# Two narrow attentions of a four-layer block: one opening stage instead of two, rows restacked through memory, dummy matmuls at the head

## The chip, the cores and the metric

The kernel runs on one core of a Trainium2 chip. Its time is the device time of one execution in microseconds (us); lower is better. Five engines work side by side: TensorE (PE, matmuls into PSUM), VectorE (DVE), ScalarE (ACT), GpSimd (POOL) and SyncE (SP), which here issues nearly all the transfers. They wait for one another on semaphores; transfers (DMAs) run on the core's 16 DMA engines.

## The reference, cut to what matters

Four layers follow one another on x (8 batches, 256 rows, 128 columns); each is an attention over a context of 64 rows and then a feed-forward part with experts. The change touches the attentions of layers 0 and 2 alone, which have 16 heads of depth 8:

```python
z = layernorm(x)                       # 2048 rows of 128
q = z @ wq + bq                        # 8 x 256 x 128
k, v = ctx @ wk + bk, ctx @ wv + bv    # 8 x 64 x 128
p = softmax(q_h @ k_h.T / sqrt(8) + mask)   # for each of 16 heads; only layer 0 has a mask
x = x + concat_h(p @ v_h) @ wo + bo
```

## The kernel before

The program is a row of blocks. All engines meet at the end of a block; a block ends when each engine has issued its last instruction, and for SP that is the issue of its last DMA, not its landing.

**Normalisation** (`normalise`): DVE takes the statistics of 16 tiles of 128 rows (L134 to L145), ACT the roots, DVE writes normalised tiles in four groups of four (L167), TensorE transposes them (L228), and ACT copies them into `zT` (L202). Layer 0 has then a small block for the context, the mask and converted constants (L2704 to L2745).

**Projection and restacking** (`project_small`): TensorE makes k for all batches and q in four groups of 512 columns (L327, L330), then v (L333). A value is carried as a high part in a rounded format and a low part, the rest: ACT writes the high part (L341, L344), DVE the low part (L350, L355). So that one matmul adds three products, high and low parts must lie one above the other on 96 partitions, for each subset of four heads. SP restacks them with DMAs from on-chip memory to on-chip memory of 32 rows by 512 columns (64 KB) each, line L308: four subsets by three parts make 12 for k and 12 for each group of q, 60 in all. They go out one by one on SP's queue.

**Attention** (`attend_small`): a new block. DVE first clears and fills constant parts (`zeroed`, L561 to L573), and TensorE and ACT wait for it. POOL spreads k of a batch over a block pattern `kbd` (L407) and adds the output bias to x (L413). Then, for batch b, TensorE runs a schedule written out by hand: scores (L423 with the mask of layer 0, L427), from which DVE takes row maxima (L580); the maxima are turned (L437) and written by ACT into rows 96 to 127 of q (L517); the turned scores (L449, L453) come out less their maxima, and ACT exponentiates them (L526); values (L466) of batch b-2 run beside that; DVE divides (L596, L598), TensorE turns and projects (L474, L478), DVE adds to x (L606). Batch b waits for the restacked q of its group (`q_there`), and for its `kbd`.

Of the kernel before, what the change touches and what calls it, by code (L numbers as in the profile page):

```python
# [21 lines left out]
P = 128  # L22
# [251 lines left out]

class Stacked:
# [7 lines left out]
    def __init__(self, m):  # L283
# [4 lines left out]
        self.k_there = m.sem("k_there")  # L288
        self.q_there = [m.sem(f"q_there{g}") for g in range(GROUPS)]


def project_small(nc, tag, w, zT, ctx2T, st, v2_all):

    with ExitStack() as stack:
        m = Memory(nc, stack, tag)
        pq = [m.ps(f"pq{i}") for i in range(GROUPS)]
        pk = m.ps("pk")
        pv = m.ps("pv", 1024)
        q_done, k_done, v_done, k_high_ready, k_low_ready, q_high_ready, q_low_ready = (
            m.sem(n) for n in ("q_done", "k_done", "v_done", "k_high_ready", "k_low_ready", "q_high_ready",  # L300
                               "q_low_ready"))
        block = stack.enter_context(nc.Block())

        @block.sync
        def _(sp):
            def restack(out, src, cols, row, there):
# [4 lines left out]
            every = slice(0, B * KEYS)  # L311
            sp.wait_ge(k_high_ready, 1)
            restack(st.k, st.k_high, every, 0, st.k_there)
            restack(st.k, st.k_high, every, 64, st.k_there)
            sp.wait_ge(k_low_ready, 1)
            restack(st.k, st.k_low, every, 32, st.k_there)
            for g in range(GROUPS):
                cols = slice(g * 512, (g + 1) * 512)
                sp.wait_ge(q_high_ready, g + 1)
                restack(st.q, st.q_high, cols, 0, st.q_there[g])  # L320
                restack(st.q, st.q_high, cols, 32, st.q_there[g])
                sp.wait_ge(q_low_ready, g + 1)
                restack(st.q, st.q_low, cols, 64, st.q_there[g])

        @block.tensor
        def _(pe):
            nc.tensor.matmul(pk[:, :].rearrange("p (b k) -> p b k", k=KEYS), w["wk"][:, :], ctx2T[:, :, 0, :],  # L327
                             start=True, stop=True).then_inc(k_done, 1)
            for g in range(GROUPS):
                nc.tensor.matmul(pq[g][:, :], w["wq"][:, :], zT[:, g * 512:(g + 1) * 512],  # L330
                                 start=True, stop=True).then_inc(q_done, 1)
# [2561 lines left out]
```

## Time and profile before

| | us |
|---|---|
| median of 3 runs | 1666.53 |
| lowest and highest run | 1655.84, 1669.77 |
| profiled execution, its own time | 1663.92 |
| its span, first to last instruction | 1662.1 |

TensorE is busy for 77% of the span, DVE for 60%, ACT for 43%, POOL for 37%; the mean granted TensorE clock is 0.84 of full speed. Two stretches are of interest: from 0 to 152 us the opening and the attention of layer 0, and from 907 to 1062 us the same of layer 2. In a row of the timeline the first number is the start in us from the span's start, the second how long the group lasted; xN counts instructions; the bracket tells how long the engine was idle before, and what released it. One matmul on plain f32 operands is recorded as two.

### The profile page before, as it was taken

To read this page: it belongs to the slowest core of one execution; us is meant where nothing else is said; L and a number is where in the kernel's file an instruction comes from. 1 tells how busy PE (TensorE), PEld (TensorE's weight loads), DVE (VectorE), ACT (ScalarE), POOL (GpSimd) and SP (SyncE) were. 2 spreads that over 40 slices of the span, in tenths; PEclk is the share of its full clock that TensorE was granted. 3 is DMA by queue.
4 is the path that set the end of the run, shared out by engine and by line. 5 is a ranking of instruction groups with operands and counts; after the bars stand their busy time and mean duration, and the time that the engine had idled before them with its cause. 6 is when DMAs were issued, how large, how long until landed. Compare 5 with 4: busy or idle time off the path is not lost. (4 is left out here: it accounts for less than half of the span.)

```text
span 1662.1 us, 24143 instructions
## 1 busy us (share of the span) xinstructions
PE 1282.1 (77%) x7118; PEld 1055.1 (63%) x7118; DVE 995.0 (60%) x2089; ACT 722.9 (43%) x1277; POOL 614.7 (37%) x566
## 2 busy tenths in 40 slices
PE   3297569998897899704994269699966549999997
PEld 2296348987654599703883159578854437787876
DVE  4255668887425377552665143568767776677775
ACT  2043446666332555322562123355542225555554
POOL 0231454432000133164331031149945306666765
PEclk9598869999798899856997555789985659999998
DMA  4530011110000000231112300022212106444433
GB/s 96 170 54 1 1 34 38 38 38 5 1 1 0 20 1 0 76 102 44 47 47 56 79 16 1 20 78 83 82 58 79 40 4 141 116 125 117 127 117 103
DMA packets 75841, 93.63 MB, mean 56 GB/s; under 512 B 16346, under 2 KB 42333, under 8 KB 75754
## 3 DMA queue, kind: packets, MB, share of 16 engines
q1 hardware_dynamic: 73154, 87.85, 18.9%
q0 software_dynamic: 2272, 4.24, 0.8%
q8 instruction: 38, 0.62, 0.2%
q10 hardware_dynamic: 336, 0.59, 0.1%
q14 instruction: 41, 0.34, 0.1%
HBM read 70.01 MB, written 8.92 MB: 47 GB/s over the span
## 5 line engine op out<-in xcount | busy, mean ns | idle before, releaser
L2485 POOL TENSOR_TENSOR e_h<-e_h,e_gate 128x512 f32<-128x512 f32 x128 | 188.1, 1487 | 144.6 <-DVE e_h L2537 87.3
L2542 DVE TENSOR_TENSOR e_h_low<-e_h,e_h_high 128x512 fp32r<-128x512 f32 x132 | 117.7, 891 | 77.7 <-ACT e_h_high L2472 77.5
L2472 ACT ACTIVATE e_h_high<-e_h 128x512 fp32r<-128x512 f32 x132 | 83.5, 633 | 103.6 <-POOL e_h L2485 95.8
L407 POOL TENSOR_TENSOR t_kbd<-a_k,groupmask 96x1024 fp32r<-96x1024 f32 x16 | 31.2, 1950 | 213.5 <-PE t_ps_t L453 80.9
L228 PE MATMUL n_ps_t<-ident,n_zn 128*128 128x128 f32 x128 | 34.4, 433 | 89.9 <-DVE n_zn L167 82.0
L1130 PE MATMUL u_ps_o<-u_vaug,u_pT 128*128 128x72 f32 x768 | 96.9, 269 | 0.0
L2537 DVE TENSOR_TENSOR e_h<-e_s,e_ps_b 128x512 f32<-128x512 f32 x132 | 89.2, 677 | 10.4 <-ACT e_s L2457 5.8
L1130 PEld LDWEIGHTS u_ps_o<-u_vaug,u_pT 128*128 128x128 f32 x768 | 93.4, 192 | 0.0
L2457 ACT ACTIVATE e_s<-e_ps_a 128x512 f32<-128x512 f32 x132 | 77.6, 588 | 25.4 <-PE e_ps_a L1493 22.8
L1061 POOL TENSOR_TENSOR u_kbd<-u_keys,groupmask 96x512 fp32r<-96x512 f32 x60 | 62.9, 1069 | 62.1 <-DMA u_keys<-s_k 36.8
L228 PEld LDWEIGHTS n_ps_t<-ident,n_zn 128*128 128x128 f32 x128 | 23.9, 224 | 97.6 <-DVE n_zn L167 77.5
L1157 ACT ACTIVATE u_sm<-u_sm 128x512 f32<-128x512 f32 x96 | 60.6, 631 | 53.4 <-DVE u_sm L1189 52.7
L1187 DVE TENSOR_REDUCE u_mx<-u_ps_s 128x2 f32<-128x512 f32 (+1 forms) x96 | 66.2, 689 | 20.7 <-PE u_ps_s L1112 19.9
L466 PE MATMUL t_ps_o<-t_vaug,t_pT 128*128 128x72 f32 x512 | 76.7, 315 | 0.0
L466 PEld LDWEIGHTS t_ps_o<-t_vaug,t_pT 128*128 128x128 f32 x512 | 75.1, 232 | 0.0
L1189 DVE TENSOR_TENSOR u_sm<-u_ps_s,u_mx 128x512 f32<-128x512 f32 x96 | 66.4, 692 | 7.1
L1933 POOL DMA_INDIRECT sorted_y<-e_y,e_zb x39 | 37.9, 972 | 88.1 <-DVE e_y L2138 86.0
L517 ACT ACTIVATE a_q<-t_ps_m 32x1024 fp32r<-32x1024 f32 x16 | 16.3, 1017 | 110.7 <-PE t_ps_m L437 110.7
L689 POOL MEMSET t_vbd<- 128x1024 f32 x1 | 1.0, 952 | 170.9 <-POOLq L626 170.9
L1709 ACT ACTIVATE e_s<-e_ps_a 128x512 f32<-128x512 f32 x64 | 38.3, 599 | 58.2 <-PE e_ps_a L1493 58.2
L427 PE MATMUL t_ps_s<-t_kbd,a_q 96*128 96x256 f32 x128 | 32.3, 369 | 40.5 <-DVE t_kbd L573 39.8
L702 POOL TENSOR_TENSOR t_sm<-t_sm,t_den 128x1024 f32<-128x1024 f32 x16 | 30.4, 1903 | 82.3 <-DVE t_den L814 82.3
(455 smaller groups left out, 3983.5 us busy)
## 6 DMA issues: line engine op xcount, KB each, us to landing
e_gate<-gates_by_expert SPq DMA_DIRECT2D x256, 128.0 KB, 3.1
e_gate<-gates_by_expert SPq DMA_DIRECT2D x32, 256.0 KB, 3.3
w_raw<-in_L1w SPq DMA_DIRECT2D x24, 256.0 KB, 4.2
a_q<-a_q_high SPq DMA_DIRECT2D x64, 64.0 KB, 2.0
u_qs<-s_q SPq DMA_DIRECT2D x16, 192.0 KB, 2.6
u_keys<-s_k SPq DMA_DIRECT2D x8, 384.0 KB, 3.5
w_w<-in_L2w SPq DMA_DIRECT2D x24, 128.0 KB, 2.7
sorted<-blank SPq DMA_DIRECT2D x1, 2535.0 KB, 17.2
```

What stands on the lines that cost most here:

```text
L228: last = nc.tensor.transpose(ps_t[g % 2][:, j * P:(j + 1) * P], normal(g * GROUP + j), ident)
L466: last = nc.tensor.matmul(ps_o[:, a * NA:(a + 1) * NA], pT[b % 2][:, j, t * P:(t + 1) * P], vaug[b % 2][:, a, pair * NA:(pair + 1) * NA], ...
L1061: return eng.tensor_tensor(kbd[:, HG * g:HG * (g + 1), kb * P:(kb + 1) * P], keys[:, kb, g, :].unsqueeze(1).broadcast_to([ROWS, HG, P]), g ...
L1130: last = nc.tensor.matmul(ps_o[par][:, a * NA:(a + 1) * NA], pT[(r - 3) % 2][:, i, :], vaug[kb][:, a, own * NA:(own + 1) * NA], start=own ...
L1157: nc.scalar.activation(sm[r % 3][:, :], sm[r % 3][:, :], ACT.Exp, scale=scale).then_inc(p_ready, 1)
L1187: nc.vector.tensor_reduce(mx[r % 2][:, 0:heads], s3, X, ALU.max)
L1189: nc.vector.tensor_tensor(sm[r % 3][:, :].rearrange("p (h k) -> p h k", h=heads), s3, mx[r % 2][:, 0:heads].unsqueeze(2).broadcast_to([P, ...
L2457: nc.scalar.activation(s[c % 3][:, :], ps_a[c % 3][:, :], ACT.Silu).then_inc(s_ready, 1)
L2472: nc.scalar.activation(h_parts[k % 3][0][:, :], h[k % 3][:, :], ACT.Copy).then_inc(high_ready, 1)
L2485: nc.gpsimd.tensor_tensor(h[c % 3][:, :], h[c % 3][:, :], gate[pair % SLOTS][:, :], ALU.mult)\
L2537: nc.vector.tensor_tensor(h[c % 3][:, :], s[c % 3][:, :], ps_b[c % 3][:, :], ALU.mult)\
L2542: nc.vector.tensor_tensor(h_parts[k % 3][1][:, :], h[k % 3][:, :], h_parts[k % 3][0][:, :], ALU.subtract).then_inc(low_ready, 1)
```

## The change

`normalise` and `project_small` (for layer 0 also the small block for the context and the mask) become one block, `open_small`, in which k is made ahead of the normalised rows and each group of q follows its transposes. Restacking goes through memory: SP stores the high and the low part whole (128 rows by 512 columns, 256 KB, L312 of the changed kernel), waits until both have landed, and fetches the three stacked parts with one DMA each (32 rows by 4 subsets by 512 columns, 256 KB, L319). Clearing and filling constants moves from DVE at the attention's start to POOL in `open_small`. `keep_busy` issues 8 matmuls on a matrix of ones in bf16 (512 columns each) into the PSUM bank `ps_o` at the attention's start, and 8 more after the scores of batch 0; nothing reads them. Loads for layer 0's context and k go out ahead of its other loads.

```diff
+def keep_busy(nc, bank, ones, times):
+    for _ in range(times):
+        nc.tensor.matmul(bank[:, :].rearrange("p (a c) -> p a c", c=P), ones,
+                         ones.unsqueeze(1).broadcast_to([P, 4, P]), start=True, stop=True)
...
+        self.v2 = m.sb("v2", [P, B, D])
+        self.kbd = [m.sb(f"kbd{i}", [P, SUBSETS, HG, KEYS], F32R) for i in range(3)]
+        self.vaug = [m.sb(f"vaug{i}", [P, 2, 4 * (NA + 2 * HD)]) for i in range(2)]
+        self.mxs = [m.sb(f"mxs{i}", [P, TPB, P], F32R) for i in range(2)]
+        self.zeros = m.sb("zeros", [P, TPB, P])
+        self.k_stored, self.k_there = m.sem("k_stored"), m.sem("k_there")
+        self.q_stored = [m.sem(f"q_stored{g}") for g in range(GROUPS)]
...
+    def store(self, sp, dram, part, src, cols, stored):
+        sp.dma_start(dram[part][:, cols], src[:, cols].bitcast(F32)).then_inc(stored, 16)
+    def fetch(self, sp, dram, out, cols, stored, there):
+        sp.wait_ge(stored, 32)
+        for row, part in ((0, 0), (32, 0 if out is self.q else 1), (64, 1 if out is self.q else 0)):
+            src = dram[part].rearrange("(s r) c -> r s c", r=32)[:, :, cols]
+            sp.dma_start(out[row:row + 32, :, cols].bitcast(F32), src).then_inc(there, 16)
...
+def open_small(nc, tag, x, ident, root, zT, w, st, ctx2T, groupmask, takes, loads=None, arrived=None, ident_loaded=None,
+               first=None):
...
+            if loads is not None:
+                loads(sp)
-                for s in range(SUBSETS):
-                    sp.dma_start(out[row:row + 32, s, cols].bitcast(F32), src[32 * s:32 * s + 32, cols].bitcast(F32))\
-                        .then_inc(there, 16)
+            st.store(sp, st.k_dram, 0, st.k_high, every, st.k_stored)
+            st.store(sp, st.k_dram, 1, st.k_low, every, st.k_stored)
+            st.fetch(sp, st.k_dram, st.k, every, st.k_stored, st.k_there)
+            for g in range(GROUPS + 1):
+                if g < GROUPS:
+                    sp.wait_ge(q_high_ready, g + 1)
+                    st.store(sp, st.q_dram, 0, st.q_high, cols(g), st.q_stored[g])
+                    sp.wait_ge(q_low_ready, g + 1)
+                    st.store(sp, st.q_dram, 1, st.q_low, cols(g), st.q_stored[g])
+                if g > 0:
+                    st.fetch(sp, st.q_dram, st.q, cols(g - 1), st.q_stored[g - 1], st.q_there[g - 1])
+        @block.gpsimd
+        def _(pool):
+            nc.gpsimd.memset(st.zeros[:, :, :], 0.0)
+            for i in range(2):
+                nc.gpsimd.memset(st.vaug[i][:, :, :], 0.0)
+            pool.drain()
+            for i in range(2):
+                nc.gpsimd.tensor_copy(st.mxs[i][:, :, :], st.zeros[:, :, :])
+            if first is not None:
+                pool.wait_ge(*first["loaded"])
+            for i in range(2):
+                for half in range(2):
+                    rows = slice(64 * half, 64 * half + 64)
+                    for pair in range(4):
+                        c = pair * NA + 8 * HD + 2 * pair + half
+                        pool.drain()
+                        nc.gpsimd.memset(st.vaug[i][rows, :, c:c + 1], 1.0)
+            for i in range(3):
+                pool.drain()
+                nc.gpsimd.tensor_copy(st.kbd[i][ROWS:P, :, :, :].rearrange("p s h k -> p (s h) k"),
+                                      takes[ROWS:P, :].unsqueeze(2).broadcast_to([P - ROWS, HEADS, KEYS]))
+            pool.drain()
         @block.vector
         def _(dve):
...
             dve.wait_ge(k_high_ready, 1)
             nc.vector.scalar_tensor_tensor(out=st.k_low[:, :], in0=pk[:, :], scalar=w["bk"][:, 0:1], in1=st.k_high[:, :],
                                            op0=ALU.add, op1=ALU.subtract).then_inc(k_low_ready, 1)
+                if g % 2 == 0:
+                    half = g // 2
+                    h = slice(half * HALF, (half + 1) * HALF)
+                    dve.wait_ge(std_ready, half + 1)
+                    nc.vector.reciprocal(rstd[:, h], std[:, h])
+                    dve.drain()
+                if g >= 2:
+                    dve.wait_ge(turned, g - 1)
+                for j in range(GROUP):
+                    t = g * GROUP + j
+                    last = nc.vector.tensor_scalar(zn[g % 2][:, j, :], x[:, t, :], mean[:, t:t + 1], rstd[:, t:t + 1],
+                                                   ALU.subtract, ALU.mult)
+                last.then_inc(normed, 1)
+                if g == 2 and first is None:
+                    low_q(0)
...
+            if first is None:
+                high_k()
+                root_of(0)
...
+            for g in range(GROUPS):
+                act.wait_ge(turned, g + 1)
+                nc.scalar.activation(zT[:, cols(g)], ps_t[g % 2][:, :], ACT.Copy).then_inc(evacuated, 1)
+                if g >= 2:
+                    high_q(g - 2)
+            for g in range(GROUPS - 2, GROUPS):
+                high_q(g)
...
+            def project_q(g):
+                pe.wait_ge(evacuated, g + 1)
+                if g == 3:
+                    pe.wait_ge(q_low_ready, 1)
+                nc.tensor.matmul(pq[g % 3][:, :], w["wq"][:, :], zT[:, cols(g)], start=True, stop=True).then_inc(q_done, 1)
...
+            project_k()
+            if first is None:
+                project_v()
+            turn(0)
+            turn(1)
+            if first is None:
+                project_q(0)
+                turn(2)
+                project_q(1)
+                turn(3)
+            else:
+                turn(2)
+                turn(3)
+                pe.wait_ge(*first["loaded"])
+                project_q(0)
+                project_q(1)
+            project_q(2)
+            project_q(3)
...
+def attend_small(nc, tag, x, w, st, ident, ident_r, groupmask, scale, ones_b, mask=None, loads=None):
...
-            pe.wait_ge(zeroed, 1)
+            keep_busy(nc, ps_o, ones_b, 8)
...
+                if b == 0:
+                    keep_busy(nc, ps_o, ones_b, 8)
...
-            nc.vector.memset(zeros[:, :, :], 0.0)
-            for i in range(2):
-                nc.vector.memset(vaug[i][:, :, :], 0.0)
-            dve.drain()
-            for i in range(2):
-                nc.vector.tensor_copy(mxs[i][:, :, :], zeros[:, :, :])
-                for half in range(2):
-                    rows = slice(64 * half, 64 * half + 64)
-                    for pair in range(4):
-                        c = pair * NA + 8 * HD + 2 * pair + half
-                        last = nc.vector.memset(vaug[i][rows, :, c:c + 1], 1.0)
-            for i in range(3):
-                last = nc.vector.tensor_copy(kbd[i][ROWS:P, :, :, :].rearrange("p s h k -> p (s h) k"),
-                                             takes[ROWS:P, :].unsqueeze(2).broadcast_to([P - ROWS, HEADS, KEYS]))
-            last.then_inc(zeroed, 1)
...
-        first = [(ctx_rows, A["ctx"].rearrange("(t p) d -> p t d", p=P)),
-                 (takes, A["takes"]), (eye2, A["eye2"]), (mask0, A["mask0"].rearrange("(t p) k -> p t k", p=P))]
-        first += [(t, A["L0" + k]) for k, t in small0.items()]
+        soonest = [(ctx_rows, A["ctx"].rearrange("(t p) d -> p t d", p=P)), (small0["wk"], A["L0wk"]),
+                   (small0["bk"], A["L0bk"])]
+        first = [(t, A["L0" + k]) for k, t in small0.items() if k not in ("wk", "bk")]
+        first += [(takes, A["takes"]), (eye2, A["eye2"]), (mask0, A["mask0"].rearrange("(t p) k -> p t k", p=P))]
...
-        normalise(nc, "n0_", x, idn, root_ln, zT, arrived=x_loaded, ident_loaded=ident_loaded, then=ACT.Exp,
-                  loads=load(first, first_loaded))
...
+            open_small(nc, "n0_", x, idn, root_ln, zT, small0, st, ctx2T, groupmask[:, :], takes[:, :], loads=first_loads,
+                       arrived=x_loaded, ident_loaded=ident_loaded,
+                       first={"loaded": (first_loaded, 16 * len(first)), "ctx_loaded": (soonest_loaded, 16 * len(soonest)),
+                              "ctx_rows": ctx_rows, "ctxT": ctxT, "hides": hides, "hidesT": hidesT,
+                              "mask": mask0[:, :, :], "prepare": prepare})
...
-        normalise(nc, "n6_", x, idn, root_ln, zT, then=ACT.Exp)
-            project_small(nc, "p2_", small2, zT, ctx2T, st, v2_all)
-            attend_small(nc, "t2_", x, small2, st, v2_all, idn, ident_r[:, :], groupmask[:, :], takes[:, :], HD ** -0.5)
+            st = Stacked(ml, q_dram, k_dram)
+            open_small(nc, "n6_", x, idn, root_ln, zT, small2, st, ctx2T, groupmask[:, :], takes[:, :])
+            attend_small(nc, "t2_", x, small2, st, idn, ident_r[:, :], groupmask[:, :], HD ** -0.5, ones_b[:, :])
```

SP's queue in layer 0's opening. Before, each DMA is of 64 KB; `a_k` and `a_q` are the stacked tensors:

```order
L304 UNCONDITIONAL_BRANCH
L308 DMA a_k<-a_k_high 32x512 x8
L308 DMA a_k<-a_k_low 32x512 x4
L308 DMA a_q<-a_q_high 32x512 x8
L308 DMA a_q<-a_q_low 32x512 x4
```

and the last two rows come three times more. Now (`k_part` and `q_part` are the tensors in memory), 25 DMAs in place of 60:

```order
L312 DMA k_part<-a_k_high 128x512
L312 DMA k_part<-a_k_low 128x512
L319 DMA a_k<-k_part 32x4x512 x3
L312 DMA q_part<-a_q_high 128x512
L312 DMA q_part<-a_q_low 128x512
L312 DMA q_part<-a_q_high 128x512
L312 DMA q_part<-a_q_low 128x512
L319 DMA a_q<-q_part 32x4x512 x3
L312 DMA q_part<-a_q_high 128x512
L312 DMA q_part<-a_q_low 128x512
L319 DMA a_q<-q_part 32x4x512 x3
```

The fetches of a group stand behind the stores of the next one; only those of the last group have nothing between.

TensorE from the transposes of the normalisation to the head of layer 0's attention, before:

```order
L228 MATMUL n_ps_t<-ident,n_zn 128x128 x16
L98 UNCONDITIONAL_BRANCH
L2710 UNCONDITIONAL_BRANCH
L2714 MATMUL su_ps_c<-ident,ctx_rows 128x128 x4
L2718 MATMUL su_ps_m<-ident,hides 128x128 x2
L2704 UNCONDITIONAL_BRANCH
L325 UNCONDITIONAL_BRANCH
L327 MATMUL p_pk<-ctx2T,L0wk 128x512
L330 MATMUL p_pq<-zT,L0wq 128x512 x4
L333 MATMUL p_pv<-L0wv,ctx2T 128x128 x8
L294 UNCONDITIONAL_BRANCH
L415 UNCONDITIONAL_BRANCH
```

and now:

```order
L538 MATMUL n_pv<-ident,ctx_rows 128x128 x4
L511 MATMUL n_pk<-ctx2T,L0wk 128x512
L525 MATMUL n_ps_t<-ident,n_zn 128x128 x16
L532 MATMUL n_pq<-zT,L0wq 128x512 x4
L563 MATMUL n_pk<-ident,hides 128x128 x2
L516 MATMUL n_pv<-L0wv,ctx2T 128x128 x8
L341 UNCONDITIONAL_BRANCH
L614 UNCONDITIONAL_BRANCH
L282 MATMUL t_ps_o<-ones_b 128x512 x8
L622 MATMUL t_ps_s<-wide_eye,hidesT 128x512
L626 MATMUL t_ps_s<-a_kbd,a_q 128x256 x2
```

k has moved ahead of the transposes, two block ends are gone, and eight dummies stand ahead of the first scores.

DVE at the attention's start, before; these rows are gone from DVE, and the first instruction in its block is now the reduction of the scores:

```order
L561 MEMSET t_zeros 128x256
L563 MEMSET t_vaug 128x704 x2
L566 CAST t_mxs<-t_zeros 128x256
L571 MEMSET t_vaug 64x2 x8
L566 CAST t_mxs<-t_zeros 128x256
L571 MEMSET t_vaug 64x2 x8
L573 CAST t_kbd<-takes 32x1024 x3
L580 TENSOR_REDUCE t_mx<-t_ps_s 128x8 x4
```

They stand on POOL now, in `open_small`.

## Rows read from the trace of the kernel before

**Rows 1.** The page's first line: span and instructions.

```profile
span 1662.1 us, 24143 instructions
```

**Rows 2.** Timeline of SP's restacking: first of layer 0, last of either layer.

```profile
25.64 5.05 SPq L308 DMA_DIRECT2D a_k<-a_k_high  x8
...
61.47 2.49 SPq L308 DMA_DIRECT2D a_q<-a_q_low  x4
...
958.41 2.49 SPq L308 DMA_DIRECT2D a_q<-a_q_low  x4
```

**Rows 3.** Timeline: start of layer 0's attention.

```profile
67.50 3.85 DVE L573 CAST t_kbd<-takes 32x1024 fp32r<-32x1024 f32 x3
...
71.41 0.80 PE L423 MATMUL t_ps_s<-wide_eye,hidesT 128*128 128x512 f32 x1 [40.16 <-DVE t_kbd L573]
```

**Rows 4.** Timeline: start of layer 2's attention.

```profile
961.58 1.89 POOL L407 TENSOR_TENSOR t_kbd<-a_k,groupmask 96x1024 fp32r<-96x1024 f32 x1 [68.34 <-SPq L377]
...
968.59 1.22 PE L427 MATMUL t_ps_s<-t_kbd,a_q 96*128 96x256 f32 x4 [39.82 <-DVE t_kbd L573]
```

**Rows 5.** Stretches: busy of PE, PEld, DVE, ACT, POOL, then clock, DMA share, GB/s.

```profile
34.00:64.00 30.00, 0.00 (x0) 0.00 (x0) 0.00 (x0) 0.00 (x0) 0.00 (x0) 0.50 0.42 103
71.00:78.00 7.00, 6.45 (x20) 5.19 (x20) 4.57 (x9) 0.02 (x1) 3.34 (x4) 0.50 0.93 319
...
84.00:100.00 16.00, 15.72 (x118) 14.74 (x117) 8.22 (x21) 7.67 (x16) 5.43 (x6) 0.97 0.72 122
```

**Rows 6.** DMA issues: what, count, KB each, median us from issue to landing.

```profile
a_q<-a_q_high SPq DMA_DIRECT2D x64, 64.0 KB, 2.0
...
sorted<-blank SPq DMA_DIRECT2D x1, 2535.0 KB, 17.2
...
out<-x SPq DMA_DIRECT2D x1, 1024.0 KB, 5.1
```

**Rows 7.** Timeline: normalisation and projection of layer 2, layer 0's tiles first.

```profile
10.71 2.14 DVE L167 TENSOR_SCALAR n_zn<-x,n_mean,n_rstd 128x128 f32<-128x128 f32 x8
...
912.05 2.14 DVE L167 TENSOR_SCALAR n_zn<-x,n_mean,n_rstd 128x128 f32<-128x128 f32 x8
...
917.73 0.60 ACT L202 ACTIVATE zT<-n_ps_t 128x512 f32<-128x512 f32 x1 [0.43 <-PE n_ps_t L228]
...
920.18 2.05 PE L327 MATMUL p_pk<-ctx2T,L2wk 128*128 128x512 f32 x2 [2.49 <-PEq L98]
...
923.97 0.69 ACT L344 ACTIVATE a_q_high<-p_pq,L2bq 128x512 fp32r<-128x512 f32 x1 [1.02 <-PE p_pq L330]
```

**Rows 8.** Timeline: a later normalisation, with POOL busy beside it.

```profile
1069.51 4.55 DVE L167 TENSOR_SCALAR n_zn<-x,n_mean,n_rstd 128x128 f32<-128x128 f32 x8
```

**Rows 9.** Stretches in layer 2, PE alone: busy, granted clock, DMA share, GB/s.

```profile
922.00:926.00 4.00, 4.00 (x8) 0.66 0.20 49
926.00:930.00 4.00, 2.77 (x19) 1.00 0.42 104
...
1030.00:1034.00 4.00, 4.00 (x22) 0.50 0.02 4
...
1038.00:1042.00 4.00, 3.49 (x31) 1.00 0.00 0
```

**Rows 10.** Timeline: one ACT step a batch in layer 2's attention (five of eight).

```profile
973.68 1.02 ACT L517 ACTIVATE a_q<-t_ps_m 32x1024 fp32r<-32x1024 f32 x1 [45.97 <-PE t_ps_m L437]
...
1018.26 1.02 ACT L517 ACTIVATE a_q<-t_ps_m 32x1024 fp32r<-32x1024 f32 x1 [1.56 <-PE t_ps_m L437]
1031.00 1.02 ACT L517 ACTIVATE a_q<-t_ps_m 32x1024 fp32r<-32x1024 f32 x1 [1.56 <-PE t_ps_m L437]
1041.33 1.02 ACT L517 ACTIVATE a_q<-t_ps_m 32x1024 fp32r<-32x1024 f32 x1 [0.74 <-PE t_ps_m L437]
1048.34 1.02 ACT L517 ACTIVATE a_q<-t_ps_m 32x1024 fp32r<-32x1024 f32 x1 [0.26 <-PE t_ps_m L437]
```

**Rows 11.** Groups by line and shape: a bf16 matmul of 512 columns.

```profile
L1112 PE MATMUL u_ps_s<-causal_b,ident_b 128*128 128x512 bf16 x32 | 13.6, 424 | 0.0
```

More of the change, by code:

```diff
@@ L294, in project_small @@
     with ExitStack() as stack:
         m = Memory(nc, stack, tag)
[L296 to L301, printed above, removed]
+        stats = m.sb("stats", [P, TILES, 6])
+        sum2, dif, ssq, mean, dif2, var, std, rstd = (m.sb(n, [P, TILES]) for n in (
+            "sum2", "dif", "ssq", "mean", "dif2", "var", "std", "rstd"))
@@ L302, in project_small @@
         block = stack.enter_context(nc.Block())
+        cols = lambda g: slice(g * 512, (g + 1) * 512)
+        every = slice(0, B * KEYS)
         @block.sync
         def _(sp):
-            def restack(out, src, cols, row, there):
-                for s in range(SUBSETS):
-                    sp.dma_start(out[row:row + 32, s, cols].bitcast(F32), src[32 * s:32 * s + 32, cols].bitcast(F32))\
-                        .then_inc(there, 16)
-            every = slice(0, B * KEYS)
+            if loads is not None:
+                loads(sp)
@@ L325, in _ @@
[L325 to L331, printed above, removed]
-            for b in range(B):
-                last = nc.tensor.matmul(pv[:, b * D:(b + 1) * D],
-                                        ctx2T[:, b, :, :].rearrange("p a k -> p (a k)"),
-                                        w["wv"][:, :], start=True, stop=True)
-            last.then_inc(v_done, 1)
@@ L338, in _ @@
-        @block.scalar
-        def _(act):
-            act.wait_ge(k_done, 1)
-            nc.scalar.activation(st.k_high[:, :], pk[:, :], ACT.Identity, bias=w["bk"][:, 0:1]).then_inc(k_high_ready, 1)
-            for g in range(GROUPS):
-                act.wait_ge(q_done, g + 1)
-                nc.scalar.activation(st.q_high[:, g * 512:(g + 1) * 512], pq[g][:, :], ACT.Identity,
-                                     bias=w["bq"][:, 0:1]).then_inc(q_high_ready, 1)
+            st.store(sp, st.k_dram, 1, st.k_low, every, st.k_stored)
@@ new lines, in _ @@
+                if g >= 2:
[7 more added lines that the diff above has]
+                    low_q(0)
+            if first is not None:
+                dve.wait_ge(*first["loaded"])
+                for i in range(2):
+                    last = nc.vector.tensor_scalar(first["hides"][:, :, i, :], first["mask"], -1.0e9 * HD ** 0.5, None,
+                                                   ALU.mult)
+                last.then_inc(hidden, 1)
+                low_q(0)
@@ L358, in _ @@
+            for g in range(1, GROUPS):
+                low_q(g)
+            if first is not None:
+                first["prepare"](dve)
+                hidesT = first["hidesT"]
+                dve.wait_ge(hides_high, 1)
+                nc.vector.tensor_tensor(hidesT[KEYS:P, :], pk[KEYS:P, 0:PAIR], hidesT[KEYS:P, :], ALU.subtract)\
+                    .then_inc(hides_low, 1)
             dve.wait_ge(v_done, 1)
-            nc.vector.tensor_tensor(v2_all[:, :, :], pv[:, :].rearrange("p (b d) -> p b d", d=D),
+            nc.vector.tensor_tensor(st.v2[:, :, :], pv[:, :].rearrange("p (b d) -> p b d", d=D),
```

195 lines of the change are left out of this document (121 added, 74 removed).

## The prediction, made before the changed kernel was run

> **What bounds the kernel now.** I read the timeline of the two openings first, then the stretches with their clock, then the DMA view. The span is 1662.1 us [rows 1]; the profiled execution took 1663.9, and the median of the three runs, 1666.5, lies 2.6 above it. The sum below is made against 1663.9.
>
> In both layers SP's queue is what the kernel waits for between projection and attention. Its 60 DMAs follow one another from 25.64 to 61.47 + 2.49 = 63.96 us in layer 0, and to 960.90 in layer 2 [rows 2]: 38.3 us, or 0.64 each. From 34 to 64 us no engine computes, and the DMA engines are at a share of 0.42 with 103 GB/s [rows 5]: what limits is the issue of small transfers, not the moving of bytes. Then comes a second wait: TensorE idles until DVE's last setup copy [rows 3, 4], so that the first scores stand at 71.41 and 968.59, which is 7.45 and 7.69 us after SP's last issue.
>
> Inside the attention TensorE decides, and its clock with it. In layer 2 the clock is at 0.5 (1.2 GHz) from 1030 to 1034 with TensorE busy all the time, and at 1.00 (2.4 GHz) from 1038 on [rows 9]. The step that comes once a batch follows after 12.74 us at the low level (1018.26 to 1031.00) and after 7.01 at the high one (1041.33 to 1048.34) [rows 10]. Layer 0, whose mask matmuls stream more columns, is at the high level from 85 us on [rows 5].
>
> **The change, part by part.**
>
> *Restacking, layer 2.* The block starts at the same time. DVE now puts the low part of k ahead of the tiles, which moves them by about 0.8 us from 912.05; TensorE puts the first q matmul (about 1.8 us at the low clock: k's, of the same shape, took 2.05 with its fill [rows 7]) ahead of the third group of transposes. So the third `zT` comes out near 919.5, the high part of q's first group at 920.4 (before: 923.97 + 0.69 [rows 7]), its low part at 921.2, and the last low part near 926.8. For q SP issues 8 stores and 12 fetches, at the 0.64 us of the old DMAs [rows 2] 12.8 us. Its first two groups wait for ACT and DVE until 924.5; 15 DMAs follow, 9.6 us, and between the last store and the last fetches lies one landing, 2.0 us from the row of 64 KB [rows 6], hardly covered, so SP ends near 936.5. Bytes: 5.24 MB for q (8 stores and 12 fetches of 0.26 MB). At the 319 GB/s of a loading stretch with share 0.93 [rows 5] they take 16.4 us, and a store of 1 MB took 5.1 us, 3.1 beyond a landing of 2.0, or 338 GB/s [rows 6]. That is level with SP's own time: 920.4 + 16.4 = 936.8. I take 936.7, so 24.2 us sooner.
>
> *Restacking, layer 0.* k now needs only the context and goes ahead, but DVE waits for its high part before it normalises: tiles from 10.71 [rows 7] to about 13.5. The four q matmuls follow all transposes, first high part near 21.6. From there the same chain of 16.2 us gives 37.8; with the gaps differently laid out I take 37.0 instead of 63.96: 27.0 sooner. The two block ends that go are within both numbers.
>
> *Setup.* DVE's setup leaves the attention's start. POOL does it in the opening, where it is idle, with over 25 us of room. What remains from block end to first scores is 0.7 us (960.90 to 961.58 [rows 4]) and the longer of POOL's first `kbd`, 1.89 [rows 4], and the eight dummies. A bf16 matmul of 512 columns takes 0.42 [rows 11], so 8 take 3.4 at the low clock. 4.1 instead of 7.45 and 7.69: 3.4 and 3.6 us.
>
> POOL beside a normalisation is not free: eight tiles took DVE 4.55 us in a later one and 2.14 here [rows 7, 8]. POOL's work here is mostly clears. Bounds 0 and 2.4 us for each attention; I take 0.5, 1 in all.
>
> *Second eight dummies.* They stand between the scores of batch 0 and 1, where TensorE waits for DVE's maxima. At the low clock they cost up to 3.4 us in each attention, at the high one half of that, which the wait covers: 0.
>
> *The clock.* The eight dummies stream 512 columns without a gap. The nearest row is the projection: plain matmuls of 512 columns from 920.18 on, and the clock rises between 922 and 926 [rows 7, 9]. If the dummies do the same, at the start or at the second eight, layer 2's attention runs at the high level throughout. Its seven steps from 973.68 to 1048.34 took 74.7 us [rows 10]. The last, 7.01, has no scores of a next batch in it; a full one I put at 7.4. At the high level: 5.7 for the first, 5 of 7.4, and 7.0: 49.7. That is 25.0 less; 1 goes to a head that is still low. 24 us. Layer 0 had only its first two batches at the low level: 3 us. The ends are 0 and 28.
>
> The Trainium skill says, in TensorE: Matmul & The Clock Gate (Part 1, the HAM clock gate), that the low clock is the default and that matmul activity releases it. By that rule taken simply, layer 2 would have risen by itself soon after 983 us, and the dummies would give it next to nothing; the row of 1030 to 1034 [rows 9] speaks against so simple a reading.
>
> The sum: layer 0 27.0 + 3.4, layer 2 24.2 + 3.6, less 1 for POOL, make 57.2; the clock 24 + 3. 1663.9 - 84.2 = 1579.7, say **1580**.
>
> **Rivals.**
>
> *The clock rises and falls again, or rises late.* Between the dummies and the first values (batch 2's turn) TensorE waits for ACT and DVE in every step, and at twice the speed it waits for a larger share. After a stretch with little work the clock fell within the idle time after 930, and stayed low for 100 us [rows 5, 9]. Then about half of the 24 is lost: 1592.
>
> *The dummies do not lift it in layer 2.* Eight make only 3.4 us, and TensorE at 4.00 of 4 busy stayed at 1.2 GHz [rows 9]. What counts is then not busy time, and a matrix of ones may not be what counts either. Then 27 is gone, and the second eight cost 3 in layer 2 and 1 in layer 0, where the clock then rises some batches in, as before: 1580 + 31 = 1611.
>
> *Slower: the transfers, not their issue, are the limit.* If the 103 GB/s of the restacking [rows 5] is what such rows of 2 KB reach, q's 5.24 MB take 50.9 us instead of 16.4. That is 34 us more in each attention, TensorE is cold in both, and the time is 1611 + 68 = 1679. It decides where the rate is below 5.24 MB / (16.4 + 28) = 118 GB/s. A store of many short rows stood at 2.6 MB in 15.2 us beyond its landing, 171 GB/s [rows 6]. Against it: share 0.42 at 103 GB/s, and 319 GB/s seven us later.
>
> The Trainium skill has a rule that speaks against this change: in DMA: Bandwidth & Descriptors, on the anatomy of a DMA, most of the fixed 2 us is the receipt from the target, and memory is the slowest target. No row gives a landing of a 256 KB store. The change waits for one five times per attention. Four of the five are behind other stores.
>
> If a landing took 4 us instead of 2.0, k's wait and the last one would cost 2 each, in both attentions: 8 us, within the range.
>
> **How the numbers follow.** High clock throughout 0.55 (1580), rise late or fall 0.20 (1592), not lifted 0.22 (1611), transfers at the limit 0.03, of which 0.01 is slower. The three runs before lie 14 us apart, which this clock can explain and which widens each case by some 7. The likeliest case's own range is 1568 to 1592. Range 1568 to 1614: below it are the case of 1580 with a shorter chain, and above it the worst of the third and the fourth, together under 0.2. What this kernel's measurement can tell from no change is about 1%, here 17 us; all of the first three cases are over 3% faster. Faster 0.97, same 0.02, slower 0.01.
>
> **What would show it.** In the changed trace: SP's last fetch near 37 and 937; the first scores near 41 and 941, behind the dummies and not behind SP or POOL; a landing of the stores near 2 to 3 us; a DMA share over 0.8 while q is stored and fetched; a clock of 1.00 in layer 2's attention and a step each 7.4 us. Wrong would be: SP waiting on landings between all groups; POOL's setup ending after SP's last fetch, so that POOL sets the block's end; a step of 12.7 us in layer 2; or layer 0's attention slower by more than a step, since the weights for the next stage load beside it.

## The result, and the profile after

| | before | changed |
|---|---|---|
| median, us | 1661.18 (4 runs, 1652.35 to 1669.77) | 1607.42 (4 runs, 1601.34 to 1612.95) |
| ratio, with its 95% interval | | 0.9676 [0.9606, 0.9746] |
| profiled execution, us | 1663.92 | 1601.34 |

The kernel is faster by 3.2%. The forecast was 1580, the range 1568 to 1614. One more execution of the kernel before, 1652.35, joined the three shown with its profile. The profiled executions are 62.6 us apart. By stage, in us from the span's start:

| | before | changed | gained |
|---|---|---|---|
| layer 0: start to first scores | 71.41 | 43.23 | 28.2 |
| layer 0: first scores to next normalisation | 81.4 | 81.05 | 0.3 |
| from there to layer 2's opening | 753.9 | 756.3 | -2.3 |
| layer 2: opening, to first scores | 61.9 | 38.0 | 23.9 |
| layer 2: attention | 94.1 | 83.3 | 10.7 |
| rest | | | 1.8 |

52 of the 63 us come from the openings. The clock, of which 27 were expected, gave about 11.

The page's first line answers to [rows 1]; below it the line on memory traffic of the changed kernel, and then that of the kernel before:

```profile
span 1599.5 us, 24144 instructions
...
HBM read 77.87 MB, written 14.16 MB: 58 GB/s over the span
...
HBM read 70.01 MB, written 8.92 MB: 47 GB/s over the span
```

The trip through memory writes 5.24 MB more in both attentions together, and reads 7.86 MB more.

Stretches of the changed kernel, with the columns of [rows 5]: six us from the end of layer 0's opening and the last twelve of layer 2's.

```profile
31.00:34.00 3.00, 0.00 (x0) 0.00 (x0) 0.00 (x0) 0.00 (x0) 0.00 (x0) 0.50 1.06 311
34.00:37.00 3.00, 0.00 (x0) 0.00 (x0) 0.00 (x0) 0.00 (x0) 0.00 (x0) 0.50 1.05 272
...
903.00:906.00 3.00, 0.00 (x0) 0.00 (x0) 0.00 (x0) 0.00 (x0) 0.00 (x0) 0.62 0.91 197
906.00:909.00 3.00, 0.00 (x0) 0.00 (x0) 0.00 (x0) 0.00 (x0) 0.00 (x0) 0.50 1.06 311
909.00:912.00 3.00, 0.00 (x0) 0.00 (x0) 0.00 (x0) 0.00 (x0) 0.00 (x0) 0.50 1.04 285
912.00:915.00 3.00, 0.00 (x0) 0.00 (x0) 0.00 (x0) 0.00 (x0) 0.00 (x0) 0.50 1.02 248
```

Still no engine computes there, but the share has gone from 0.42 to above 0.9 (a few stretches read slightly over 1) and the rate from 103 GB/s to between 197 and 311. The limit has moved from SP's issues to the transfers. The DMA issues of 880 to 920 us show it again, with the columns of [rows 6]:

```profile
a_q<-q_part SPq DMA_DIRECT2D x12, 256.0 KB, 6.0
q_part<-a_q_high SPq DMA_DIRECT2D x4, 256.0 KB, 3.8
q_part<-a_q_low SPq DMA_DIRECT2D x4, 256.0 KB, 4.4
a_k<-k_part SPq DMA_DIRECT2D x3, 256.0 KB, 4.2
k_part<-a_k_high SPq DMA_DIRECT2D x1, 256.0 KB, 2.0
```

k's first store, with nothing beside it, lands after 2.0 us; those of q, which share the engines with fetches, after 3.8 and 4.4. What SP waited for in the same stretch (us in total, times, longest):

```profile
SPq L312 <- ACT a_q_high L478: 8.1, 2, 5.5
SPq L319 <- DMA q_part<-a_q_low: 5.8, 2, 3.3
```

And the timeline at the end of layer 2's opening:

```profile
906.34 0.44 SPq L312 DMA_DIRECT2D q_part<-a_q_low  x1
909.30 5.80 SPq L319 DMA_DIRECT2D a_q<-q_part  x6
...
915.53 1.89 POOL L323 TENSOR_TENSOR a_kbd<-a_k,groupmask 96x1024 fp32r<-96x1024 f32 x1 [25.52 <-SPq L583]
915.54 3.57 PE L282 MATMUL t_ps_o<-ones_b 128*128 128x512 bf16 x8 [15.41 <-PEq L341]
...
918.55 1.41 PE L626 MATMUL t_ps_s<-a_kbd,a_q 96*128 96x256 f32 x4
...
921.51 3.24 PE L282 MATMUL t_ps_o<-ones_b 128*128 128x512 bf16 x8
```

A single store's issue takes 0.44 us, but the last six fetches take 5.80 together, 0.97 each, while the DMA engines are full. The last store of q is issued at 906.34; the last fetch is issued by 915.10. The first scores follow the eight dummies directly (918.55), and no longer wait for a setup.

Stretches of PE alone in layer 2's attention, with the columns of [rows 9]:

```profile
916.00:924.00 8.00, 7.64 (x22) 0.50 0.38 80
924.00:931.00 7.00, 4.38 (x28) 0.98 0.00 0
931.00:961.00 30.00, 29.57 (x136) 0.50 0.00 1
962.00:1001.00 39.00, 34.38 (x279) 1.00 0.00 1
```

The clock rises right behind the second eight dummies, is at 0.98 for seven us in which PE is busy for only 4.38, falls, and stays at 0.50 for 30 us with PE busy all the time. The step that comes once a batch (the answer to [rows 10]) shows the price:

```profile
925.43 1.02 ACT L718 ACTIVATE a_q<-t_ps_m 32x1024 fp32r<-32x1024 f32 x1 [23.01 <-PE t_ps_m L636]
931.16 1.02 ACT L718 ACTIVATE a_q<-t_ps_m 32x1024 fp32r<-32x1024 f32 x1 [2.05 <-PE t_ps_m L636]
943.00 1.02 ACT L718 ACTIVATE a_q<-t_ps_m 32x1024 fp32r<-32x1024 f32 x1 [1.56 <-PE t_ps_m L636]
955.74 1.02 ACT L718 ACTIVATE a_q<-t_ps_m 32x1024 fp32r<-32x1024 f32 x1 [1.56 <-PE t_ps_m L636]
965.89 1.02 ACT L718 ACTIVATE a_q<-t_ps_m 32x1024 fp32r<-32x1024 f32 x1 [0.74 <-PE t_ps_m L636]
973.38 1.02 ACT L718 ACTIVATE a_q<-t_ps_m 32x1024 fp32r<-32x1024 f32 x1 [0.74 <-PE t_ps_m L636]
```

5.73 at first, then 11.84, 12.74 and 10.15, then 7.49. Where PE stood idle before the clock fell, the timeline shows:

```profile
926.50 0.74 PE L652 MATMUL t_ps_t<-a_q,a_kbd 128*128 128x256 f32 x4 [1.11 <-ACT a_q L718]
...
928.90 1.31 DVE L771 CAST a_mxs<-t_mx 128x32 fp32r<-128x32 f32 x1
...
930.69 0.44 PE L636 MATMUL t_ps_m<-ident_r,a_mxs 128*128 128x128 f32 x2 [1.32 <-DVE a_mxs L773]
```

PE waits 1.11 us for ACT and 1.32 for DVE. The cast at 928.90 took 1.31 us; the same one at 922.53 took 0.28. A `kbd` of POOL (928.28, 1.89 us) runs beside the long one. Whether these waits made the clock fall, this one trace does not show; the next execution has them too.

### The profile page after: what moved, and what is told of

It reads as the page before. It is cut to its first block and busy times, and to the rows that moved or that the text cites. A ratio compares the mean times of both kernels' runs of the same rounds, so it can differ in the third digit from the quotient of the medians.

```text
span 1599.5 us, 24144 instructions
## 1 busy us (share of the span) xinstructions
PE 1274.2 (80%) x7150; PEld 1040.9 (65%) x7150; DVE 984.1 (62%) x2041; ACT 721.8 (45%) x1276; POOL 627.5 (39%) x614
## 5 line engine op out<-in xcount | busy, mean ns | idle before, releaser
L323 POOL TENSOR_TENSOR a_kbd<-a_k,groupmask 96x1024 fp32r<-96x1024 f32 x16 | 30.3, 1891 | 110.0 <-PE t_ps_t L652 68.8
L665 PE MATMUL t_ps_o<-a_vaug,t_pT 128*128 128x72 f32 x512 | 70.2, 297 | 0.0
L764 DVE TENSOR_REDUCE t_mx<-t_ps_s 128x8 f32<-128x512 f32 x64 | 41.2, 685 | 46.0 <-PE t_ps_s L626 45.8
L228 PE MATMUL n_ps_t<-ident,n_zn 128*128 128x128 f32 x96 | 25.5, 429 | 55.0 <-DVE n_zn L167 47.2
L665 PEld LDWEIGHTS t_ps_o<-a_vaug,t_pT 128*128 128x128 f32 x512 | 68.4, 215 | 0.0
L1337 ACT ACTIVATE u_pT<-u_ps_t 128x512 f32<-128x512 f32 x96 | 57.2, 596 | 8.2 <-PE u_ps_t L1302 6.4
L1675 PE MATMUL e_ps_y<-e_h_high,ed_low 128*128 128x512 f32 x132 | 53.0, 401 | 8.4 <-DVE e_y L2730 5.4
```

Of the source, the lines that this page charges most:

```text
L665: last = nc.tensor.matmul(ps_o[:, a * NA:(a + 1) * NA], pT[b % 2][:, j, t * P:(t + 1) * P], vaug[b % 2][:, a, pair * NA:(pair + 1) * NA], ...
L1337: nc.scalar.activation(pT[r % 2][:, :, :].rearrange("p a b -> p (a b)"), ps_t[r % 2][:, :], ACT.Copy).then_inc(pT_ready, 1)
```

## The experiments

The theory after the result: the trip through memory saves SP's issues, though the transfers then set the openings' end; and the dummies lift the clock for a moment only, since PE waits for ACT and DVE right after them. The rivals: the dummies give most of the gain of the attention, or nothing of the gain comes from the trip through memory (merging alone would do). Kernels named a and e1 to e3 shared the runs of the kernel before on one chip (17 executions, median 1657.37), e4 to e7 on another (11, median 1657.23).

**The changed kernel again.** 

> The changed kernel once more, as the neighbour of the next three on the same chip. Ratio to the kernel before 0.968 (0.961 to 0.975 so far). In its trace the clock of layer 2's attention rises with the second eight dummies (924 us), falls at 931 and rises again at 962. If that pattern belongs to the kernel, the rise at the second eight comes again, within some 4 us of it, and the single times lie within 1.5% of one another; if it is chance, layer 2's attention is at the low level here from its start, or at the high level throughout, and its length differs from 83.3 us by more than 10.

Measured: median 1604.48 of six (1581, 1592, 1603, 1606, 1612 and 1626), ratio 0.9665 [0.9606, 0.9724]. The profiled execution was the lowest, 1581.37, and in it the forecast's likeliest case stands, a clock high throughout. PE from its first scores on:

```profile
915.00:924.00 9.00, 6.46 (x36) 1.00 0.03 7
924.00:932.00 8.00, 6.61 (x56) 1.00 0.00 0
932.00:961.00 29.00, 26.47 (x219) 1.00 0.01 2
```

and the steps:

```profile
925.36 1.02 ACT L718 ACTIVATE a_q<-t_ps_m 32x1024 fp32r<-32x1024 f32 x1 [2.05 <-PE t_ps_m L636]
932.16 1.02 ACT L718 ACTIVATE a_q<-t_ps_m 32x1024 fp32r<-32x1024 f32 x1 [0.73 <-PE t_ps_m L636]
939.65 1.02 ACT L718 ACTIVATE a_q<-t_ps_m 32x1024 fp32r<-32x1024 f32 x1 [0.74 <-PE t_ps_m L636]
```

Layer 2's attention lasts 68.8 us against 83.3 in the other execution of the same instructions. That difference, 14.5, is most of the 20.0 between the two. The clock's course is thus not fixed by the program: ten executions lie between 1581 and 1626. PE's waits behind the dummies are here as well, 1.11 us for ACT at 920.70 and, at the turn of batch 1's maxima,

```profile
924.88 0.44 PE L636 MATMUL t_ps_m<-ident_r,a_mxs 128*128 128x128 f32 x2 [1.31 <-DVE a_mxs L773]
```

and the clock does not fall at them. They are thus no sufficient cause of a fall.

**e1: without the dummies.**

```diff
-            keep_busy(nc, ps_o, ones_b, 8)
...
-                if b == 0:
-                    keep_busy(nc, ps_o, ones_b, 8)
```

> The changed kernel without its 32 dummy matmuls. Theory: they lift the clock for a few us only, because after them TensorE waits for DVE and ACT and the clock falls again; they cost 1.6 us at each head (3.5 against POOL's 1.9). Then layer 2's attention runs at 1.2 GHz from its first scores on until some later batch, lasts some 6 us longer than the 83.3 us with them, and the time is about that of the changed kernel, 1600 to 1612. Rival A, the dummies are what makes the later rise at 962 come: then layer 2's attention stays low for most of its batches as in the kernel before, 94 us, and the time is 1612 to 1620. Rival B, the dummies do nothing for the clock: first scores 1.6 us sooner in each layer, the rest the same, 1600 to 1604.

Measured: 1604.5, ratio 0.9676 [0.963, 0.9722], against 0.9665 with them. The 16 dummies of each attention give nothing that can be measured on the median; the intervals would hide some 10 us. Without them the six executions lie within 11 us (1600.68 to 1611.42), and none is as low as the two lowest with them, 1581 and 1592. In the profile the first scores of layer 2 stand 1.2 us sooner after the opening's start (36.8), and the low level lasts longer:

```profile
931.00:974.00 43.00, 42.36 (x193) 0.50 0.00 1
975.00:1005.00 30.00, 26.43 (x215) 1.00 0.00 1
```

The attention took 89.9 us, 6.5 more than 83.3, as expected. Rival A (1612 to 1620) is out; rival B (1600 to 1604) is not told apart by the time, but the first step of layer 2's attention, 7.20 us in place of 5.73, shows that the dummies do lift the clock for a moment.

**e2: the old restacking inside the new opening.** SP issues the 60 DMAs on chip again; POOL and PE wait for 12 of them each.

```diff
-            st.store(sp, st.k_dram, 0, st.k_high, every, st.k_stored)
-            st.store(sp, st.k_dram, 1, st.k_low, every, st.k_stored)
-            st.fetch(sp, st.k_dram, st.k, every, st.k_stored, st.k_there)
+            restack(st.k, st.k_high, every, 0, st.k_there)
+            restack(st.k, st.k_high, every, 64, st.k_there)
...
```

> The changed kernel with the old way of restacking in the new opening: 60 DMAs of 64 KB each from on-chip memory to on-chip memory, nothing through memory. Theory: what the trip through memory buys is SP's issue time, and part of it is given back since the transfers themselves fill the DMA engines (share 1.0 in the changed kernel). 48 q DMAs at 0.63 us from 895.8 in layer 2 end near 926, against 915.1: 11 us more in each layer, time 1607 + 22 = 1629. The share of the DMA engines then stands near 0.42. Rival, the trip is worth all and merging the stages nothing: 19 us more in each layer, 1645 or above. Rival, the trip is worth nothing: the time stays within 5 us of the changed kernel's.

Measured: 1628.72, ratio 0.9793 [0.9735, 0.985], so 24.2 us over the changed kernel's 1604.5 on the same chip. The profiled execution, 1634.48, was the longest of the six, and 766 us lie between its two attentions, 10 more than in the changed kernel's (e7 has the same, and the stage it comes from); only its openings are compared: layer 2's took 49.2 us against 38.0, layer 0's first scores stand at 56.92 against 43.23. The end of layer 2's opening:

```profile
940.70 5.02 SPq L367 DMA_DIRECT2D a_q<-a_q_high  x8
945.76 2.49 SPq L367 DMA_DIRECT2D a_q<-a_q_low  x4
948.93 1.89 POOL L323 TENSOR_TENSOR a_kbd<-a_k,groupmask 96x1024 fp32r<-96x1024 f32 x1 [36.77 <-SPq L586]
```

SP issues without a gap at 0.63 a DMA, as in [rows 2], and the share stands at 0.42 from 925 to 940, as expected. The trip through memory is worth 11.2 + 13.7 = 24.9 us in the openings, which is the whole difference of the medians. Of the 52 us that the openings gained, 27 remain in this run (56.92 and 49.24 against 71.41 and 61.9 before), from merging the stages and moving the setup; e4 puts the setup's part at 2.7, and no run tests merging alone. Both rivals are out.

**e3: the kernel before, with the dummies alone**, 8 ahead of `zeroed` and 8 after batch 0's scores.

> The kernel before with the 16 dummy matmuls at each attention's head and nothing else; the first eight lie behind DVE's setup there. Theory: they lift the clock for a few us, at the second eight; layer 2's attention (94.1 us before) changes by -12 to +3, layer 0's by -3 to +2; ratio to the kernel before 0.992 to 1.002. Rival, the dummies hold the clock in a batch that follows a long idle stretch: layer 2's attention takes 70 us, ratio 0.985. Rival, no effect on the clock: the second eight cost 3 us in each, ratio 1.003.

Measured: median 1660.71 of twelve, ratio 0.9997 [0.9966, 1.0028]: nothing. In layer 2 the clock does not rise behind them:

```profile
969.00:976.00 7.00, 3.21 (x11) 0.50 0.01 4
976.00:1018.00 42.00, 38.81 (x167) 0.50 0.00 0
```

That attention took 85.8 us, since the clock came up two batches earlier than in the execution before (94.1). In layer 0 it did rise behind them and fell again: the first two steps are 6.72 and 9.98 us.

**e4: the setup back on DVE**, at the attention's start, with the waits for it; POOL's block in the opening is gone.

```diff
-        @block.gpsimd
-        def _(pool):
-            nc.gpsimd.memset(st.zeros[:, :, :], 0.0)
...
+            pe.wait_ge(zeroed, 1)
```

> The changed kernel with the setup of constants back on DVE at each attention's start. Theory: the setup's 7.0 us lie again between the block's end and the first scores, less the 3.5 us that the dummies take there: first scores 3 to 4 us later in each layer, time 1607 + 7 = 1614. In return POOL no longer blocks DVE while layer 2's tiles are normalised (3.93 us for eight tiles in the changed kernel, 2.14 alone), but the transfers set the end of that block, so this gives back 1 us at most. Rival: the dummies hide it wholly, 1607 or below.

Measured: 1615.04, ratio 0.9735 [0.9677, 0.9794] (one of the four executions took 4348 us and is not in the ratio; why is not known). The interval overlaps that of the changed kernel, so the median alone does not settle it. The profile has both sides: the head waits for DVE,

```profile
919.45 3.85 DVE L754 CAST a_kbd<-takes 32x1024 fp32r<-32x1024 f32 x3
923.35 0.74 PE L605 MATMUL t_ps_s<-a_kbd,a_q 96*128 96x256 f32 x4 [3.43 <-DVE a_kbd L754]
```

7.0 us from block end to first scores in place of 3.0; but the opening's block ends 3.3 us sooner in layer 2 (31.7 us from its start, against 34.7 to 35.0 in three executions with the setup on POOL), and in layer 0 at 38.5 against 40.2 and, in the second execution of the changed kernel, 39.1. For layer 2 a cause is in the changed kernel's timeline, DVE's first eight tiles in layer 2 and what POOL does beside them:

```profile
886.93 3.93 DVE L441 TENSOR_SCALAR n_zn<-x,n_mean,n_rstd 128x128 f32<-128x128 f32 x8
...
886.51 3.51 POOL L398 CAST a_kbd<-takes 32x1024 fp32r<-32x1024 f32 x3
```

3.93 in place of 2.14 [rows 7]. The Trainium skill says in SBUF — State Buffer (Who interferes with whom) that VectorE, in the modes that a `tensor_scalar` can take, and GpSimd contend for one pair of ports, and that the second to issue is blocked until the first is done; the row agrees, with 1.8 us over eight tiles. q's first high part is ready 12.7 us after the opening's start here and 15.3 in the changed kernel, so 2.6 of the 3.3 us lie ahead of q's restacking. In layer 0 POOL's small clears (from 17.22, 3.93 us) ran beside DVE's second eight tiles (17.64), and these took 2.14 us as alone; the 0.6 to 1.7 us there have no cause in the tiles and stay open. Net, moving the setup gained 0.75 us in layer 2 and 2.0 in layer 0.

**e5: the fetches of q's last two groups go out in the attention's block**, so that the opening ends with the last store.

```diff
-                if g > 0:
+                if 0 < g <= 2:
...
+            for g in (2, 3):
+                st.fetch(sp, st.q_dram, st.q, slice(g * 512, (g + 1) * 512), st.q_stored[g], st.q_there[g])
```

> The changed kernel, but the fetches of q's last two groups are issued from the attention's block, ahead of its loads, where batches 4 and 6 are the first to need them. Theory: the opening ends when SP has issued the last fetch, and SP waits there for stores that lie behind full DMA engines; without these six fetches it ends after the last store, at 906.8 in place of 915.1 in layer 2 and at 31.5 in place of 39.8 in layer 0. 8 us in each, 16 in all: 1591; the clock's chance of some 10 us to either side stays. Rival: the transfers themselves are what the attention needs, so the first scores (group 0, landed near 905) or batch 4 wait for them instead, and less than 5 us is won.

Measured: 1580.88, ratio 0.9507 [0.946, 0.9553], 24 us under the changed kernel's 1604.5 (measured on the other chip), where 16 were expected. First scores of layer 0 at 34.12 (43.23), layer 2's opening 29.2 us (38.0):

```profile
896.83 0.43 SPq L312 DMA_DIRECT2D q_part<-a_q_low  x1
897.70 3.57 PE L282 MATMUL t_ps_o<-ones_b 128*128 128x512 bf16 x8 [6.55 <-PEq L341]
899.93 5.74 SPq L319 DMA_DIRECT2D a_q<-q_part  x6
```

The six fetches need the same time, now beside the first batches. No step of either attention is longer for it by more than 0.1 us. This is the largest gain of the experiments over the changed kernel: 9.1 + 8.8 = 17.9 us in the openings; the other 6 are within the spread of the runs. The rival is out.

**e6: dummies in the gaps too**, four after the turn of batch 0's maxima, eight ahead of that of batch 1.

```diff
+                if b == 2:
+                    keep_busy(nc, ps_o, ones_b, 8)
                 if 0 <= b - 1 < B:
                     turn_max(b - 1)
+                if b == 1:
+                    keep_busy(nc, ps_o, ones_b, 4)
```

> The changed kernel with 4 more dummies after the turned maxima of batch 0 and 8 more ahead of those of batch 1, where TensorE waited for ACT and DVE before the clock fell. Theory: the clock rises at the second eight dummies and falls because TensorE has little work until the values of batch 0; with work put there it stays at 2.4 GHz, every step of layer 2's attention after the second takes 7.5 us, and that attention 69 to 72 us in each profile; time 1590 (1584 to 1596), and its single times lie closer together. Rival: the fall is not from that gap, or the extra dummies cost what they give: 1604 or more, with a step of 12.7 us somewhere.

Measured: 1586.58 (1583.24 to 1594.44), ratio 0.9572 [0.9531, 0.9613]. The clock holds:

```profile
930.00:988.00 58.00, 51.68 (x420) 1.00 0.01 1
```

The four and the eight fill PE's waits for ACT and DVE, and layer 2's attention lasts 69.0 us, as in the lucky execution above (68.8). The six executions lie within 11 us where those of the changed kernel on one chip lay 44 apart, which fits a clock that takes the same course each time; e1's six, with no dummies at all, lay as close. The rival, with its step of 12.7 us, is out.

**e7: e5 and e6 together.**

> Both edits of the two runs above together. If they are independent the gains add: 1574 (1566 to 1582), which would beat both kernels. Rival: with the fetches of q still running beside the first batches, batch 4 of either layer waits for its q, the clock falls in that gap, and the time is 1585 or more.

Measured: 1573.08 (1567.18 to 1580.35), ratio 0.9479 [0.9437, 0.9522], the best median of all. The expectation of 1574 is met, but it was the sum of an expected 16 and 17; from the measured ratios the sum would be 0.9507 + 0.9572 - 0.9665 = 0.9414, or 1560, and with intervals of half a per cent on each of them the measured 0.9479 cannot be told from that. In the profile both edits keep their effect: the openings are as short as e5's (34.45 and 29.15), and layer 2's attention takes 70.8 us (81.7 in e5), so the rival is out. The stretch between the two attentions, which no edit touches, takes 763.2 us where the others, except for e2 with 765.9, had 754 to 759. All of it lies in the stage right behind layer 0's attention (268.7 us in e7, 269.1 in e2, 258.9 to 260.7 in the rest), and there in the clock. TensorE in e7 and then in e5, of the same matmuls:

```profile
205.00:220.00 15.00, 15.00 (x66) 0.50 0.14 40
...
205.00:220.00 15.00, 15.00 (x125) 1.00 0.16 45
```

The clock rises some 17 us later in e7 and in e2. Why it does so in these two executions is open; with one profile of each kernel it can be chance.

**All profiled executions side by side.** The steps between the once-a-batch ACTIVATE, in us, show in each attention whether the clock held: a second step near 10 in layer 0, or of 10.7 and more in layer 2, has the low clock in it.

| | layer 0, first two steps | layer 2, first three steps | layer 2's attention |
|---|---|---|---|
| before (no dummies) | 8.01, 8.46 | 7.21, 11.89, 12.74 | 94.1 |
| e1 (no dummies) | 8.18, 8.44 | 7.20, 11.89, 12.74 | 89.9 |
| changed | 6.71, 10.01 | 5.73, 11.84, 12.74 | 83.3 |
| changed, again | 6.71, 8.43 | 5.73, 6.80, 7.49 | 68.8 |
| e2 | 6.72, 8.44 | 5.73, 11.73, 12.74 | 81.7 |
| e3 | 6.72, 9.98 | 7.21, 11.88, 12.74 | 85.8 |
| e4 | 6.70, 10.03 | 5.73, 10.66, 12.74 | 87.9 |
| e5 | 6.72, 10.00 | 5.73, 11.81, 12.74 | 81.7 |
| e6 (gaps filled) | 7.05, 8.45 | 5.88, 6.82, 7.49 | 69.0 |
| e7 (gaps filled) | 7.05, 8.45 | 5.89, 6.81, 7.50 | 70.8 |

With dummies at the head alone the clock stayed up behind them in 3 of 12 attentions; with the gaps filled as well, in 4 of 4. The moment of the rise does not decide: e2 and e5 rose within one or two us of layer 2's first scores and fell some ten us later, and e7 rose only six us behind its first scores (between 913 and 914) and held.

## Why the prediction came out so

**Restacking.** The mechanism was right, and e2 gives its size. SP's last fetch came 34.6 us after the opening's start in layer 2 where the forecast has 30.0, and at 39.8 in layer 0 where it has 37.0, so 4.5 and 2.8 us late. Part of that lies ahead of the chain: q's first high part was ready 15.3 us after the start, where the forecast has 13.7, and at 23.4 in layer 0, where it has 21.6. In layer 2 this is the price of POOL's setup (12.7 us in e4, without it); in layer 0 the tiles begin at 15.30, forecast 13.5. The chain itself, from that high part to the last fetch, took 19.3 and 16.4 us, forecast 16.3 and 15.4. The rate had been taken from a loading stretch, 319 GB/s [rows 5]; stores and fetches mixed came to 5.24 MB in 19.3 us, 272 GB/s. The issues cost less than the 0.64 assumed while the DMA engines had room (0.3 to 0.5) and more when they were full (0.90 and 0.97 for each of the last nine fetches of layer 2). The landing, 2.0 in the forecast, was 3.8 to 4.4 under load. The first store of k, with nothing beside it, landed after 2.0 us, as a 64 KB transfer on the chip did [rows 6]: storing to memory as such cost no longer landing here. The slower rival, 103 GB/s for such rows, is refuted by the share and the rate.

**Setup.** The head shrank as forecast (by 4.0 us in layer 2 against e4's, where 3.6 was taken), but the price of POOL's work was mis-sized: 3.3 us in layer 2 by the block end of e4, against 0.5 taken and an upper bound of 2.4 for each. It is not to be added to the lateness above, of which it is the larger part in layer 2. There POOL's casts fall on the first eight tiles. In layer 0 the same comparison gives 0.6 to 1.7.

**Second dummies.** Right in their place, but in layer 2 the clock of the first profile is still low at 921.51, and eight took 3.24 us, where the forecast has 0. With e1 the medians are equal, so what the dummies cost and what they bring cancel, to within some 10 us.

**The clock.** This is the step that failed. The median lies 27 us over the point; of the 22 us by which the profiled execution does, the clock's term makes 16 and the openings 5. "Layer 2's attention runs at the high level throughout" was given 0.55, and was seen in one of the two profiled executions of the changed kernel; the medians of 1604 and 1607, and the falls in layer 2 of e2, e4 and e5, which have the same dummies, show that it is not the typical one. The rival with 0.20, a clock that rises and falls again while PE waits for ACT and DVE, is what the other profile shows. Layer 2's attention gained 10.7 us of 24, near the half that the rival gave. The rival's 1592, with 5.1 us that the openings gained less than forecast (52.1 for 57.2), 2.7 that layer 0's attention did not gain and 1.3 more in layer 2's, is 1601; the profiled execution took 1601.3. Not only the dummies' lift but what follows them matters: e6 and e7 fill the gaps behind them, and the clock holds in all four attentions. That filling raises the chance of a held clock is what the counts show; what makes one execution of the unfilled kernel hold it and the next not is open. Nor is it shown why the clock did not rise in layer 2 of e3: PE is idle for 3.4 us behind the first eight dummies there, but it is so in e4 too, where the second eight lifted it.

The high step was forecast at 7.4 and came at 7.49. The likeliest case was 1579.7, and the execution with a high clock took 1581.4. That near a match is in part luck: its openings gained 3.9 us less than forecast, and the kernel's last part, for which nothing was forecast, came 3.0 us shorter. The range held the median because it had been opened up to 1614 for the case of dummies that do not lift the clock at all, which is not what happened in this kernel: at 924 to 931 the clock was up.

The rule that the forecast took from the Trainium skill, TensorE: Matmul & The Clock Gate (Part 1, the HAM clock gate), that matmul activity releases the low clock, fails here in its simple reading, as it did in [rows 9]: 931 to 961 has 29.57 of 30 us busy at 0.50. Another passage of the Trainium skill fits: TensorE: Matmul & The Clock Gate (Part 1, the second failure mode) tells of a kernel whose clock goes back and forth because TensorE idles briefly between groups of matmuls. The gaps of 1.11 and 1.32 us ahead of the fall, and e6 and e7 with these gaps filled, agree; the second execution, with the same gaps and no fall, shows that they do not always do it.

## What to carry to other kernels

Small on-chip transfers that are bound by their issue (share well under 1, one DMA every 0.63 us) can go through memory in large ones at a profit, but then look at which of the fetches the next stage needs first: letting a block end after the stores gave another 18 us here. The dummies at the head of a stage were worth nothing measurable by themselves; the clock held each time only where the waits right behind them were filled too (four attentions of four, against three of twelve). A term for the clock belongs in a forecast with both its cases, because the same program can show either. Work that is moved to an idle GpSimd can be paid for by VectorE where it falls beside VectorE's own tiles: here that took back 3.3 of the 4.0 us that the move had won in layer 2.

## What the runs showed of the hardware

- One program showed two courses of TensorE's clock, and with them 68.8 and 83.3 us for the same stage.
- TensorE stayed at 1.2 GHz for 43 us with 42.36 busy (e1, 931 to 974) and at 2.4 GHz for 39 us with 34.38 busy (962 to 1001 of the changed kernel): busy time alone does not tell the level.
- Two waits of TensorE of 1.1 and 1.3 us stood ahead of a fall of the clock in one execution and ahead of none in another.
- A store of 256 KB landed after 2.0 us alone and, in the median, 3.8 to 4.4 beside fetches; a fetch took 6.0.
- A DMA's issue on SP's queue took 0.3 to 0.5 us for 256 KB between chip and memory while the DMA engines had room, 0.97 for each of six when they were full, and 0.63 for 64 KB on the chip.
- Eight tiles of 128x128 took VectorE 2.14 us alone and beside GpSimd's small clears (layer 0), and 3.93 beside its casts (layer 2).
